# Two convolution attention layers: scores made twice, the second time with keys as rows, and each query's maximum added as a row of the queries

## What is computed

```python
attn = jnp.einsum('bhnd,bhmd->bhnm', q * scale, k)
rel_h = jnp.einsum('bnhwc,hkc->bnhwk', rq, Rh)
rel_w = jnp.einsum('bnhwc,wkc->bnhwk', rq, Rw)
attn = (attn.reshape(Bw, NH, WS, WS, WS, WS) + rel_h[..., :, None] + rel_w[..., None, :]).reshape(Bw, NH, N, N)
attn = jax.nn.softmax(attn, axis=-1)
out = jnp.einsum('bhnm,bhmd->bhnd', attn, v)
...
out = out @ proj_w + proj_b
```

## Time and profile before

| | us |
|---|---|
| median of 3 runs | 1468.78 (1464.65 to 1472.25) |
| the profiled execution | 1465.66 |
| its span in the profile | 1463.9 |
| L0 setup, span 11.9 to 32.6 | 20.7 |
| L0 attention stages | 62.6 and 61.4 |
| L1 attention stages | 53.5 and 53.4 |
| the four projection stages | 50.3, 48.5, 48.7 and 49.2 |

### The profile page before, as it was taken

The page is one execution under the profiler, slowest core; times in us unless marked ns, Lnnn a source line. Parts: engine busy times, 40 slices in busy tenths (PEclk is TensorE's granted clock), DMA queues, the critical chain, the costliest instruction groups (busy, mean ns, idle before and its releaser), DMA issues. The chain is left out here.

```text
span 1463.9 us, 28380 instructions
## 1 busy us (share of the span) xinstructions
PE 1138.0 (78%) x10258; PEld 801.8 (55%) x10259; DVE 665.5 (45%) x1945; ACT 441.4 (30%) x1186; POOL 94.1 (6%) x132
## 2 busy tenths in 40 slices
PE   0888889777877979897978429993697897549993
PEld 0666467644655757574637317772373473436772
DVE  6266126722652737474847602222583374431223
ACT  2244225411431435342424103330241252112220
POOL 2000000010000000000000040003100000040004
PEclk9988788877787989797969659997797998768997
DMA  7000000020000000009300231111910000021113
GB/s 191 2 3 2 1 2 3 2 79 6 3 1 2 2 1 1 1 2 190 134 1 1 54 93 43 48 47 50 210 66 0 0 1 1 1 75 47 46 48 103
DMA packets 31965, 57.24 MB, mean 39 GB/s; under 512 B 3461, under 2 KB 28678, under 8 KB 30826
## 3 DMA queue, kind: packets, MB, share of 16 engines
q1 hardware_dynamic: 28664, 48.34, 12.2%
q0 software_dynamic: 3072, 6.30, 1.5%
q10 hardware_dynamic: 114, 1.04, 0.3%
HBM read 41.80 MB, written 13.86 MB: 38 GB/s over the span
## 5 line engine op out<-in xcount | busy, mean ns | idle before, releaser
L719 ACT ACTIVATE work<-banks,nmax 128x256 f32<-128x256 f32 (+3 forms) x528 | 198.6, 427 | 196.2 <-DVE nmax L758 195.1
L638 PE MATMUL banks<-K,Q 128*28 128x196 f32 (+5 forms) x1056 | 204.5, 359 | 18.9 <-PEq L87 18.9
L758 DVE TENSOR_REDUCE nmax<-banks 128x2 f32<-128x512 f32 (+3 forms) x264 | 153.4, 581 | 100.1 <-PE banks L663 62.6
L1318 PE MATMUL banks<-gu,sxT 96*128 x496 | 177.8, 503 | 0.8 <-ACT sxT L1353 0.6
L638 PEld LDWEIGHTS banks<-K,Q 96*128 96x128 f32 (+4 forms) x1056 | 142.7, 176 | 35.4 <-issue 23.3
L214 PE MATMUL banks<-xT,weights 96*96 96x512 f32 (+3 forms) x288 | 150.2, 682 | 9.5 <-ACT xT L426 8.8
L767 DVE COPY work<-banks 128x512 f32<-128x512 f32 (+3 forms) x264 | 149.5, 566 | 10.3 <-PE banks L674 8.9
L1379 DVE TENSOR_TENSOR h<-sg,banks 128x384 f32<-128x384 f32 x62 | 34.4, 555 | 236.4 <-ACT sg L1361 236.4
L674 PE MATMUL banks<-small,work 128*128 128x128 f32 (+2 forms) x912 | 139.7, 270 | 0.0
L1318 PEld LDWEIGHTS banks<-gu,sxT 96*128 96x128 f32 x496 | 92.8, 197 | 54.5 <-issue 7.6
L674 PEld LDWEIGHTS banks<-small,work 128*128 128x128 f32 (+2 forms) x912 | 102.1, 139 | 22.9 <-ACT work L719 7.3
(11 more groups left out here) (209 smaller groups left out, 1402.4 us busy)
## 6 DMA issues: line engine op xcount, KB each, us to landing
gu<-in_L2f_gu SPq DMA_DIRECT2D x1, 6912.0 KB, 36.8
xin<-slots_in SPq DMA_DIRECT2D x62, 96.0 KB, 1.9
slots_out<-y SPq DMA_DIRECT2D x62, 96.0 KB, 1.6
gu<-in_L3f_gu SPq DMA_DIRECT2D x1, 5184.0 KB, 31.4
dn<-in_L2f_dn SPq DMA_DIRECT2D x1, 4608.0 KB, 47.8
slots_in<-zeros SPq DMA_DIRECT2D x1, 2976.0 KB, 11.3
dn<-in_L3f_dn SPq DMA_DIRECT2D x1, 2592.0 KB, 37.4
gu<-in_L2f_gu SPq DMA_DIRECT2D x1, 2304.0 KB, 13.6
```

What stands on the lines that cost most here:

```text
L638: ins = nc.tensor.matmul(S(s)[r0:r0 + rn, hh, 0:lay.width(t)], lay.q(m, t, h, win), lay.k(m, t, h, win), start=(hh == 0 or kind != "causal ...
L719: ins = nc.scalar.activation(w.Pr[0:rows, s % 3, hh, 0:lay.width(t)], S(s)[0:rows, hh, 0:lay.width(t)], ACT.Exp, bias=w.nmax[0:rows, s % 4 ...
L758: nc.vector.tensor_reduce(w.nmax[0:rows, s % 4, :], S(s)[0:rows, :, 0:lay.width(t)], AX.X, ALU.max, negate=True).then_inc(max_ready, 1)
L1318: ins = nc.tensor.matmul(banks[:, 2 + 2 * par + n, 0:EF], w.sxT[:, par, k, :], w.gu[:, bass.ds(e, 1), k, n * EF:(n + 1) * EF].rearrange("p ...
```

## The change

In L0 and L1 attend is replaced by a new function, attend_relative; the causal layers keep attend. A unit u is now an image m and a pair of heads g with all of its query tiles, 12 units in a stage.

Q has one slot for each pair of heads, with no zeros: the score matmuls contract over 64 partitions, 0 to 63 for one head and 64 to 127 for the other. The scores are made twice. The first time (scores) queries are the rows, and DVE takes the negated maxima (maxima). For three units at a time PE turns the maxima to 6 rows (turn_max), DVE copies them to SBUF (turned_maxima), and two small DMAs on SP's queue write them into row 48 and row 112 of the queries. The keys have a row of ones there (MAX_ROW in _one_hot_rows). The second time (scores_turned), five steps later, keys are the rows, so the maximum is already taken off and the tile is already turned: ACT exponentiates both heads and all queries in one instruction (exponent), straight into what weigh reads. The transposes and DVE's copies of the turned tiles are gone.

Banks: the first scores have banks 0 to 3 (L1: two units in turn; L0: one unit), the turned scores banks 4 and 5 (the last four units take 0 and 1 in turn with them), the outputs bank 6, turned maxima and other small work bank 7.

In the projection stage a pair's products are copied to Q by one engine, ACT for even pairs and DVE for odd ones, and L1's keys by one instruction for both images. In setup both memsets of Q are gone.

```diff
+MAX_ROW = 48
...
-            chain(nc.gpsimd.memset(w.Q[64:P, 0::2, :], 0.0))
...
-            chain.free(nc.vector.memset(w.Q[0:64, 1::2, :], 0.0))
...
-        def queries_out(copy, g, half):
-            rows = slice(64 * half, 64 * half + 64)
-            bank, q = banks[rows, (2 + n_vjobs + g) % 4, :], w.Q[rows, 2 * g + half, :]
+        def queries_out(copy, g):
+            bank, q = banks[:, (2 + n_vjobs + g) % 4, :], w.Q[:, g, :]
             if not windows:
                 return copy(q, bank)
...
-                    for m in range(PAIR):
-                        ins = nc.vector.tensor_tensor(w.K[:, g, m, :], src[:, m * TOKENS:(m + 1) * TOKENS],
-                                                      w.hot[:, :], ALU.add)
+                    ins = nc.vector.tensor_tensor(w.K[:, g, :, :], src.rearrange("p (m n) -> p m n", m=PAIR),
+                                                  w.hot[:, None, :].to_broadcast([P, PAIR, TOKENS]), ALU.add)
                 ins.then_inc(k_out, 1)
-            for g in range(6):
+            for g in range(1, 6, 2):
                 dve.wait_ge(a_done, 2 + n_vjobs + g + 1)
-                queries_out(nc.vector.tensor_copy, g, 1).then_inc(odd_out, 1)
-            dve.wait_ge(odd_out, 6)
+                queries_out(nc.vector.tensor_copy, g).then_inc(odd_out, 1)
+            dve.wait_ge(odd_out, 3)
...
-            for a in range(2 + n_vjobs + 6):
+            for a in [*range(2 + n_vjobs), *range(2 + n_vjobs, 2 + n_vjobs + 6, 2)]:
...
-                pe.wait_ge(a_out, a - 3)
-                if g >= 4:
-                    pe.wait_ge(odd_out, g - 3)
+                if g < 4:
+                    pe.wait_ge(a_out, a - 3)
+                elif g == 4:
+                    pe.wait_ge(a_out, 2 + n_vjobs + 1)
+                else:
+                    pe.wait_ge(odd_out, 1)
...
+def attend_relative(nc, env, w, ip, windows):
...
+    U = PAIR * HP
+    LAG = 5
+    ck = 98 if windows else P
+    tile_rows = (98, 98, 68) if windows else (P, P)
+    keys = WN if windows else TOKENS
...
+        def key_columns(n):
+            if not windows:
+                return [(0, TOKENS, 0, 0), (0, TOKENS, P, TOKENS)]
+            if n == 0:
+                return [(0, WN, 0, 0), (0, WN, 98, WN)]
+            nq = WINDOW_BOX[n][1] * WINDOW_BOX[n][3]
+            return [(WINDOW_AT[n], nq, n * WN + 98 * c, 2 * WN + 60 * c + WINDOW_AT[n] - WN) for c in range(2)]
+        window_list = range(WINDOWS) if windows else range(1)
+        def s_banks(u):
+            return 0 if windows else 2 * (u % 2)
+        def st_banks(u):
+            return 0 if u >= U - 4 and u % 2 == 0 else 4
+        def st_before(u):
+            return [v for v in range(u) if st_banks(v) == st_banks(u)][-1:]
...
+            def scores(u):
+                m, g = divmod(u, HP)
+                q, k = w.Q[:, g, m * TOKENS:(m + 1) * TOKENS], w.K[:, g, m, :]
+                if u >= (1 if windows else 2):
+                    pe.wait_ge(max_ready, u if windows else u - 1)
+                for t in range(2):
+                    for hh in range(2):
+                        r = slice(64 * hh, 64 * hh + 64)
+                        ins = nc.tensor.matmul(banks[0:ck, s_banks(u) + hh, t * keys:(t + 1) * keys],
+                                               q[r, t * ck:(t + 1) * ck], k[r, 0:keys], start=True, stop=True)
+                if windows:
+                    for n in range(1, WINDOWS):
+                        nq = WINDOW_BOX[n][1] * WINDOW_BOX[n][3]
+                        for hh in range(2):
+                            r = slice(64 * hh, 64 * hh + 64)
+                            ins = nc.tensor.matmul(banks[32 * (n - 1):32 * (n - 1) + nq, 2 + hh, 0:WN],
+                                                   q[r, WINDOW_AT[n]:WINDOW_AT[n] + nq], k[r, n * WN:(n + 1) * WN],
+                                                   start=True, stop=True)
+                ins.then_inc(scores_ready, 1)
+            def turn_max(b):
+                pe.wait_ge(max_ready, 3 * b + 3)
+                pe.wait_ge(misc_read, misc.index(("NT", b)))
+                at = 0
+                for t, rows in enumerate(tile_rows):
+                    ins = nc.tensor.transpose(banks[0:6, 7, at:at + rows],
+                                              w.nmax[0:rows, b % 2, t, :, :].rearrange("p s g -> p (s g)"),
+                                              ident[0:rows, 0:rows])
+                    at += rows
+                ins.then_inc(max_turned, 1)
+            def scores_turned(u):
+                m, g = divmod(u, HP)
+                q, k = w.Q[:, g, m * TOKENS:(m + 1) * TOKENS], w.K[:, g, m, :]
+                pe.wait_ge(max_in[u // 3], 32)
+                for v in st_before(u):
+                    pe.wait_ge(exp_ready, v + 1)
+                for n in window_list:
+                    for q0, nq, k0, at in key_columns(n):
+                        for hh in range(2):
+                            r = slice(64 * hh, 64 * hh + 64)
+                            ins = nc.tensor.matmul(banks[0:ck, st_banks(u) + hh, at:at + nq], k[r, k0:k0 + ck],
+                                                   q[r, q0:q0 + nq], start=True, stop=True)
+                ins.then_inc(st_ready, 1)
+            def weigh(G):
+                m, g = divmod(G, 3)
+                pe.wait_ge(exp_ready, 2 * G + 2)
+                if G >= 1:
+                    pe.wait_ge(O_out, G)
+                for n in window_list:
+                    for c, (q0, nq, k0, at) in enumerate(key_columns(n)):
+                        for j in range(4):
+                            u, h = 2 * G + j // 2, 4 * g + j
+                            v = w.V[0:98, m * 8 + n * 2 + c, h, :] if windows else w.V[:, m * 2 + c, h, :]
+                            ins = nc.tensor.matmul(banks[32 * j:32 * j + VW, 6, q0:q0 + nq], v,
+                                                   w.PT[0:ck, u % 3, j % 2, at:at + nq], start=(c == 0), stop=(c == 1))
+                ins.then_inc(pv_done, 1)
...
+            for s in range(U + LAG + 1):
+                if s < U:
+                    scores(s)
+                if s % 3 == 0 and 3 <= s <= U:
+                    turn_max(s // 3 - 1)
+                if LAG <= s < U + LAG:
+                    scores_turned(s - LAG)
+                if s - LAG >= 2 and (s - LAG) % 2 == 0:
+                    weigh((s - LAG) // 2 - 1)
...
+            def exponent(u):
+                act.wait_ge(st_ready, u + 1)
+                if u >= 3:
+                    act.wait_ge(pv_done, (u - 3) // 2 + 1)
+                at = st_banks(u)
+                nc.scalar.activation(w.PT[0:ck, u % 3, :, :], banks[0:ck, at:at + 2, :], ACT.Exp).then_inc(exp_ready, 1)
...
+        @block.sync
+        def _(sp):
+            for b in range(U // 3):
+                m, g0 = divmod(3 * b, HP)
+                sp.wait_ge(NT_out, b + 1)
+                for hh in range(2):
+                    row = 64 * hh + MAX_ROW
+                    sp.dma_start(w.Q[row:row + 1, g0:g0 + 3, m * TOKENS:(m + 1) * TOKENS],
+                                 w.NT[3 * hh:3 * hh + 3, b % 2, :]).then_inc(max_in[b], 16)
...
+            def maxima(u):
+                m, g = divmod(u, HP)
+                b, at = u // 3, s_banks(u)
+                dve.wait_ge(scores_ready, u + 1)
+                if u % 3 == 0 and b >= 2:
+                    dve.wait_ge(max_turned, b - 1)
+                out = w.nmax[0:ck, b % 2, 0:2, :, g % 3].rearrange("p t s -> p s t")
+                ins = nc.vector.tensor_reduce(
+                    out, banks[0:ck, at:at + 2, 0:2 * keys].rearrange("p s (t k) -> p s t k", t=2), AX.X, ALU.max, negate=True)
+                if windows:
+                    ins = nc.vector.tensor_reduce(w.nmax[0:68, b % 2, 2, :, g % 3], banks[0:68, 2:4, 0:WN], AX.X, ALU.max,
+                                                  negate=True)
+                ins.then_inc(max_ready, 1)
+            def turned_maxima(b):
+                dve.wait_ge(max_turned, b + 1)
+                if b >= 2:
+                    dve.wait_ge(max_in[b - 2], 32)
+                if windows:
+                    nc.vector.tensor_copy(w.NT[:, b % 2, 0:WN], banks[0:6, 7, 0:WN])
+                    nc.vector.tensor_copy(w.NT[:, b % 2, WN:WN + 56].rearrange("p (n q) -> p n q", n=2),
+                                          banks[0:6, 7, WN:WN + 64].rearrange("p (n q) -> p n q", n=2)[:, :, 0:28])
+                    ins = nc.vector.tensor_copy(w.NT[:, b % 2, WN + 56:TOKENS], banks[0:6, 7, WN + 64:WN + 68])
+                else:
+                    ins = nc.vector.tensor_copy(w.NT[:, b % 2, :], banks[0:6, 7, 0:TOKENS])
+                ins.then_inc(NT_out, 1)
+                dve.wait_ge(NT_out, b + 1)
+                dve.sem_inc(misc_read, 1)
...
+            for s in range(U + LAG + 1):
+                if s < U:
+                    maxima(s)
+                if s % 3 == 0 and 3 <= s <= U:
```

(22 more changed lines are left out.)

121 lines of the change are left out of this document (118 added, 3 removed).

## The result

The changed kernel takes 1480.49 us (median of 5 runs, 1474.58 to 1484.55) against 1465.94 for the kernel before, run beside it (1459.56 to 1472.25): a ratio of 1.0111, 95% interval 1.0082 to 1.0139. It is slower by 14.6 us, and I had forecast 1536, slower by 67. The profiled execution took 1474.58 us (span 1472.4), the fastest of its five, so stage lengths read from it make up 9 us of the 14.6. The page's busy line of after, against the earlier trace rows: TensorE has more instructions but less busy time, VectorE 84.5 us less, ScalarE 51 us less.

A forecast was written before the change was run, and what follows sets the result against it. PE's executed work was taken to bound each attention stage, plus start and end waits. Terms: 41.6 + 42.8 - 5.2 - 5.1 - 5.2 - 1.2 = +67.7 on 1465.7, 1533.4; forecast 1536, range 1455 to 1590.

The forecast's parts named there:

- rival B: L0 attention stages: clock at 1.00, stages +3.1 and +4.3, total 1460; a rise midway gives 1460 to 1500; chance 27%.
- L0, to the first turned scores: Start of an L0 attention stage: first scores and maxima take turns at the lower clock, first turned scores at 22.0 us.
- L0, from there to the end of the last weighing: Middle of an L0 attention stage: turned scores, first scores, weighings and outputs, 73.3 us at the lower clock.
- L0, the end: End of an L0 attention stage: as L1's, with slower matmuls and four copies of ACT instead of one, 8.9 us.
- L1 stage: Full-image attention stage: 48.3 us against 53.5 and 53.4 before, -5.2 and -5.1.
- setup L0, L1: Setup stages: memsets of Q go, -5.2 us in L0; DVE waits for an earlier PE result, -1.2 in L1.
- The step that failed: L0 attention stages: start gaps and load-bound work keep the clock at 0.50 through most of a stage, 104.2 us each.
- C: Rival: the two row groups don't run side by side; L0 stages +126, L1 stages +130, total 1790; chance 12%.
- D: Rival: matmuls pair but weight loads don't, 12 x 0.163 more a step, total 1583; chance 9%.
- F: Rival: 98-column weight loads keep some 0.08 us at the lower clock, 24 steps of 0.97 us less, 1513; chance 2%.
- E: Rival: the L1 stages stay at 0.50 as well, about 17 us each, total 1570; chance 6%.
- The projection stages: Projection stages: copies to Q halve in number but PE's products hide them, 0 us, range -1 to +1 each.

The follow-up runs named there:

- e_cold_no_small: The changed kernel without filler, L0's turned scores of the three small windows left out (output not the layer's): 1459.49 us, ratio 0.9934 to the kernel before.
- e_filler: The changed kernel plus three filler matmuls behind each of the first five units' first scores in L0: 1464.1 us, ratio 0.9994 to the kernel before.
- e_same_rows: The changed kernel with both heads taken from partitions 0 to 63, so no pairing is possible (output not the layer's): 1784.03 us, 1 run.
- e_l0_only: The change in the window layer (L0) alone, L1 as in the kernel before: 1488.99 us, ratio 1.0164 to the kernel before.
- e_banks2: The changed kernel with own banks for L0's first scores of units 1 and 3 and later normalisation: 1468.94 us, ratio 1.0008 to the kernel before.
- e_bankfill: e_banks2 plus four filler products in each of two L0 waits of PE for VectorE: 1459.35 us, ratio 0.9931 to the kernel before.

## Why the prediction was wrong in size

The sign, and the place of the loss (L0, by the clock), were right. One step failed and carried nearly all of the miss. That 1480 lies within my 1455 to 1590 is owed to rival B's times between, not to the sum.

| term | forecast | profile |
|---|---|---|
| L0, to the first turned scores | 22.0 | 23.1, 23.1 |
| L0, from there to the end of the last weighing | 73.3 (39.5 at 1.00) | 41.9, 44.7 |
| L0, the end | 8.9 | 8.7, 8.6 |
| L1 stage | 48.3 | 47.7, 48.5 |
| setup L0, L1 | -5.2, -1.2 | -5.6, -1.2 |

**The step that failed** is "So I take it that the clock stays at 0.50 through most of an L0 stage". It held for the first 23.9 and 30.0 us, the start steps, and not for the steps behind them. I took the load-bound part and the changes of mode as reasons, but the steps that hold both ran at 1.00 for 40.7 and 37.3 us. Without the load-bound matmuls the clock stays low through the start all the same (e_cold_no_small), and it rises at +4 once the waits are filled (e_filler). What ended the low stretch in both stages was the first run without a gap, as in the earlier trace rows, and I had those rows. The stretch I leaned on the earlier trace rows was one with TensorE idle half of the time; it speaks for the start steps (12.7 busy of 20.7) and says nothing on steps without a gap. The middle of the two stages was 31.4 and 28.6 us shorter than its term: 60 us, where the total's shift by the profiles was 59 less than forecast.

**Rival B** (1.00 in L0; midway, 1460 to 1500) was the case that came. Its text names the deciding point rightly, the first step in which the clock rises. Its full price of +3.1 and +4.3 for stages at the higher clock was low: e_filler, high from +4 on, has 68.3 instead of 65.7. The start fits (17.8 against 18.3), the middle is 41.8 instead of 39.5 (0.8 of it because six first scores take 1.30 us, not 1.17), and the end runs at the lower clock, 8.7 instead of 7.9. So even with the clock up, this L0 stage is 5.7 and 6.9 us longer than before, 12.6 of the 17.5 us that the setups and L1 gain in the profiles, and e_filler's median is level with before. Both parts were small against the term of the clock.

**What held.** The heads pair, matmuls and weight loads both, so C and D fall (turned unit 1.72 and 3.33 us; forecast 1.7 and 3.27). F falls with the 3.33. The 0.082 us for 98 columns of the Trainium skill (TensorE: Matmul & The Clock Gate, "LDWEIGHTS") is near the 0.088 us measured at 2.4 GHz (1.72 less four slots of 0.165, over twelve) and half of the 0.168 at 1.2: by it (an estimate), a turned unit at 1.2 GHz would take 2.3 us. My 0.163 for the lower clock divided by 16 where its twin divides by 15; by 15 it is 0.172. E falls: the L1 clock rose at +5.5 and +6.4. In L1 the first turned scores came at +11.2 (forecast 11.7), behind the one visible transfer wait of 1.6 us, and a group of scores takes 0.87 us (0.86). The exponent of 1024 columns takes 1.02 us (1.05). The start step is 4.02 us (3.85). The projection stages, for which I had 0 with a range of -1 to +1 each, moved by -2.1 to +2.3; the new code of the first L0 one took 48.0 to 52.2 us in the profiles of the runs that hold it, so one profile can't tell what the change did to it.

**The setup** gave its 5.2 us in a slightly other way. VectorE's timeline in the L0 setup, after:

```profile
13.93 2.76 DVE L107 TENSOR_SCALAR norm_v<-norm_mean_var 128x4 f32<-128x4 f32 x1
16.73 1.43 DVE L110 TENSOR_SCALAR norm_a<-norm_v 128x4 int32<-128x4 int32 x1
18.19 0.17 DVE L113 TENSOR_SCALAR norm_rstd<-norm_a 128x4 int32<-128x4 int32 x1
```

The instruction of four columns that took 2.71 us still takes 2.76, now under GpSimd's next fill. What is gone is one such fill from the row of them, so the quick instructions begin at 18.19 instead of 20.86.

**What stays open.** The rise took 3.2, 9.3, 6.0 and 15 us of gapless work in different stages, and never came in an L0 stage of e_same_rows. The runs show that both matter, waits of 0.7 to 1.6 us and whether the two heads' matmuls lie in one half of the rows or in both, but not the rule by which they add, nor why the stretch is 3.2 us in one stage and 9.3 in the next. That the medians differ by 14.6 us and the profiles by 9 fits a rise that varies between executions (e_l0_only, profiled near its median, had 76.7 and 76.4). The rise was not measured for each execution, but the mean granted clock was: 0.829 in the one of 1474.58 us and 0.822 and 0.823 in the two of 1484.3 and 1484.6.

## What to carry to other kernels

A start in which one bank group is passed back and forth costs more than its waits: here 1.6 us per step kept the clock low for 24 to 30 us of every L0 stage, and matmuls whose values nobody reads, put in those waits, gave the higher clock back and took 5 to 8 us off a stage. When you forecast a clock, price the stretch with waits and the stretch without them apart, from rows of either kind. Pairing heads in the two halves of the rows works for matmuls and weight loads, but matmuls with few columns then still pay for their weights: 0.088 us each at 2.4 GHz for 98 columns of them.

## What the hardware showed that was not expected

- TensorE busy without a gap for 110 us, with matmuls over 64 of 128 rows one at a time, stayed at 0.50 (e_same_rows). The same instructions spread over both halves saw it rise.
- With a wait of 1.6 us just before and another just behind, the clock went from 1.00 to 0.50, and it took 17 us to return (e_banks2, low from 89.1 to 106.1).
- At 0.50, one filler product a step left a wait of 0.70 in 4.03 us, and the clock rose at +24.1 and +20.4; three left none, and it rose at +4. Waits of 0.43 in steps of 2.97 us behind the rise did not bring it down.
- Filler products with only 32 columns of weights, in two waits of 1.6 us, went with a clock that stayed up, where it had fallen without them (e_bankfill, e_banks2).
